# A small local attention with 64 patch units per core, rewritten inside a four-layer kernel

## What is computed

```python
q = Wq @ qp + bq;  k = Wk @ qp + bk;  val = Wv @ vp + bv          # 64 x 128 a patch
scores = einsum('bhdi,bhdj->bhij', qh, kh) / sqrt(8)
scores = where(mask > 0, scores, -1e9);  attn = softmax(scores)
o = gelu(einsum('bhij,bhdj->bhdi', attn, vh))                     # exact gelu
out = (Wo @ o + bo) * masks
```

## Time and profile before

| | us |
|---|---|
| median of 3 runs | 3458.11 (3456.35 to 3464.62) |
| profiled execution, its own time | 3458.61 |
| its span | 3456.7 |
| PE busy | 3137.7 (91%) |
| DVE busy | 1975.3 (57%) |
| POOL busy | 1141.7 (33%) |
| ACT busy | 943.9 (27%) |

### The profile page before, as it was taken

The page is one execution under the profiler, slowest core; times in us unless marked ns, Lnnn a source line. Parts: engine busy times, 40 slices in busy tenths (PEclk is TensorE's granted clock), DMA queues, the critical chain, the costliest instruction groups (busy, mean ns, idle before and its releaser), DMA issues.

```text
span 3456.7 us, 47231 instructions
## 1 busy us (share of the span) xinstructions
PE 3137.7 (91%) x15840; PEld 2524.9 (73%) x15840; DVE 1975.3 (57%) x3823; ACT 943.9 (27%) x3176; POOL 1141.7 (33%) x935
## 2 busy tenths in 40 slices
PE   5999999999989889989989888888878999999899
PEld 4778888888768644457767677777766888888687
DVE  7555555555543454477766666666666444445643
ACT  2222222222210033310033333333322333333211
POOL 4333333433255222136621221222113322232264
PEclk9999999999999965579999999999989999999999
DMA  2111111111111000021110110110002111111011
GB/s 97 40 40 42 36 39 45 45 42 36 44 43 39 18 20 13 7 60 31 41 34 19 28 30 18 30 30 24 9 22 58 29 35 30 30 38 29 26 51 46
DMA packets 68604, 120.64 MB, mean 35 GB/s; under 512 B 7840, under 2 KB 13216, under 8 KB 68112
## 3 DMA queue, kind: packets, MB, share of 16 engines
q1 hardware_dynamic: 68496, 119.23, 11.6%
HBM read 117.11 MB, written 2.10 MB: 34 GB/s over the span
## 4 chain that ended last, share of the span: by engine, by line
PE 71%; DVE 17%; issue 6%; ACT 3%; POOL 2%; DVEq 0%; DMA 0%; POOLq 0%; ACTq 0%; SPq 0%
PE proj L341 31%; PE outp L341 18%; PE heado L823 5%; PE score L803 4%; PE score L1593 3%; PE turn L816 2%; DVE nw_t L370 2%; PE score L341 2%; DVE nw_t L368 1%; DVE tbuf L988 1%; PE turn L742 1%; ACT sq L897 1%; DVE x L1038 1%; DVE rowmax L993 1%; DVE stats L390 1%
## 5 line engine op out<-in xcount | busy, mean ns | idle before, releaser
L341 PE MATMUL outp<-w_out,acts 128*128 128x512 f32 x3288 | 867.8, 408 | 38.0 <-DVE x L1038 20.0
L341 PE MATMUL proj<-xnT,w_in 128*128 128x512 f32 x3288 | 783.5, 393 | 9.5 <-DVE big L864 3.0
L341 PEld LDWEIGHTS outp<-w_out,acts 128*128 128x128 f32 x3288 | 607.8, 193 | 176.3 <-DVE x L1038 29.4
L341 PEld LDWEIGHTS proj<-xnT,w_in 128*128 128x128 f32 x3288 | 613.8, 189 | 141.7 <-issue 6.3
L341 PE MATMUL proj<-ctxT,w_kv 128*128 128x512 f32 x2304 | 563.4, 404 | 52.9 <-DVE big L864 43.7
L341 PEld LDWEIGHTS proj<-ctxT,w_kv 128*128 128x128 f32 x2304 | 443.0, 194 | 153.6 <-DVE big L864 46.6
L602 POOL TENSOR_TENSOR w_out<-ring,consts 128x512 fp32r<-128x512 f32 x96 | 104.0, 1083 | 1039.8 <-PE outp L341 1039.8
L1038 DVE TENSOR_TENSOR x<-x,outp 128x512 f32<-128x512 f32 x384 | 261.4, 686 | 255.6 <-PE outp L341 254.1
L913 ACT ACTIVATE pbuf<-tbuf,negmax 128x128 f32<-128x128 f32 x512 | 199.2, 390 | 396.9 <-DVE negmax L995 393.9
L602 POOL TENSOR_TENSOR w_kv<-ring,consts 128x512 fp32r<-128x512 f32 x96 | 105.8, 1102 | 465.0 <-DMA ring<-in_L_wk 465.0
L864 DVE COPY big<-proj 128x512 f32<-128x512 f32 x136 | 94.0, 691 | 255.7 <-PE proj L341 255.3
(11 more groups left out here) (239 smaller groups left out, 4032.7 us busy)
## 6 DMA issues: line engine op xcount, KB each, us to landing
ring<-in_L_wq SPq DMA_DIRECT2D x96, 256.0 KB, 2.7
ring<-in_L_wo SPq DMA_DIRECT2D x96, 256.0 KB, 2.6
ring<-in_F_in SPq DMA_DIRECT2D x52, 256.0 KB, 2.6
ring<-in_L_wk SPq DMA_DIRECT2D x48, 256.0 KB, 2.7
ring<-in_L_wv SPq DMA_DIRECT2D x48, 256.0 KB, 2.8
ring<-in_F_out SPq DMA_DIRECT2D x41, 256.0 KB, 2.6
ring<-in_mask SPq DMA_DIRECT2D x16, 256.0 KB, 3.2
x<-in_x SPq DMA_DIRECT2D x2, 1024.0 KB, 7.4
```

What stands on the lines that cost most here:

```text
L341: mm = pe.matmul(bank_ap, w_ap(a, c), rhs(b, c), start=first and c == 0 and n == 0, stop=last and c == chunks - 1 and n == len(PASSES) - 1)
```

## The change

- **Scores.** q and k are projected three times over into stacks of 96 rows for each s (`wq3`, `wk3`: 4 projections a batch instead of 2). The stack holds high, high, low of q against high, low, high of k, so that one fp32r pass over 98 rows gives the score. Two rows hold the mask.
- **Softmax.** DVE takes the negated maximum, and ACT takes four exps a unit, straight from PSUM with the maximum as bias. The subtraction goes.
- **Values.** The stationary operand is a 128x128 block: 8 value rows per head on a diagonal, and 8 columns of ones. All 8 heads accumulate into one PSUM column block per patch. The result is channels by positions already, with 64 rows of values and 64 rows of sums. Turning back, copying out and per-patch scaling go; DVE takes one reciprocal of 64x512 a batch and one product of 64x512. The copies out of `turn` are shared: ACT for even units, DVE for odd.
- **Key tiles.** POOL writes 98x512 tiles for each unit into 8 buffers. It also clears the padded value blocks ahead of the stage.
- **End.** Gelu, mask (POOL) and `Wo` with its bias as row 65 go batch by batch. Nothing is turned. DVE adds once.
- **F1's start.** SP loads F1's first weights once the last batch's keys are masked. POOL splits them (`ffn_pool_first`) before its tail work. `c2` of F1 has a place of its own.
- The loops over batches are written out instead of running on a register.

The core of the diff (added lines; what is removed is in the listing above; `...` marks left-out lines; in `kraw1`, `kstk`, `qstk`, `kbd`, `v1`, `sum1` the first index after the rows is the buffer):

```diff
+        wait(pool, m["blocked"], UNITS * b)
+        for s in range(2):
+            pool.wait_ge(m["k_high"], 2 * b + s + 1)
+            pool.tensor_tensor(kstk[32:64, b % 2, s, :], kraw1[32:64, s, :], kstk[32:64, b % 2, s, :].bitcast(F32),
+                               ALU.subtract).then_inc(m["k_low"], 1)
+        pool.wait_ge(m["mask_made"], 2 * b + 2)
+        pool.wait_ge(m["k_low"], 2 * b + 2)
+        for u in range(UNITS):
+            n, s = divmod(u, 2)
+            wait(pool, m["sfull"], UNITS * (b - 1) + u + 1)
+            pool.tensor_tensor(kbd[0:ROWS, u, :].rearrange("p (h j) -> p h j", h=4),
+                               kstk[0:ROWS, b % 2, s, n * P:(n + 1) * P].bitcast(F32).unsqueeze(1)
+                               .broadcast_to([ROWS, 4, P]), heads, ALU.mult).then_inc(m["blocked"], 1)
...
+    def project_k(b, s):
         pe.wait_ge(m["normed"], b + 1)
...
+        if s == 0:
+            wait(pe, m["v_made"], b)
+        else:
+            wait(pe, m["q_low"], 2 * b)
+        pe.matmul(proj[s][0:STACK, :], wk3[:, s * STACK:(s + 1) * STACK], xn1[b % 2], start=True, stop=True)\
+          .then_inc(m["k_full"], 1)
...
+    def project_q(b, s):
+        pe.wait_ge(m["k_masked"], 2 * b + s + 1)
+        pe.matmul(proj[s][0:STACK, :], wq3[:, s * STACK:(s + 1) * STACK], xn1[b % 2], start=True, stop=True)\
+          .then_inc(m["q_full"], 1)
...
...
+    def scores(u):
+        b, n, s = u // UNITS, u % UNITS // 2, u % 2
+        pe.wait_ge(m["blocked"], u + 1)
+        pe.wait_ge(m["q_low"], 2 * b + s + 1)
+        wait(pe, m["exps"], u - 1)
+        pe.matmul(score[s][:, :], qstk[0:ROWS, b % 2, s, n * P:(n + 1) * P], kbd[0:ROWS, u % UNITS, :],
+                  start=True, stop=True).then_inc(m["sfull"], 1)
...
+    def turn_probabilities(u):
+        s = u % 2
+        pe.wait_ge(m["exps"], u + 1)
+        wait(pe, m["tfree", s], u // 2)
+        for h in range(4):
+            mm = pe.transpose(turn1[s][:, h * P:(h + 1) * P], pbuf[:, s, h * P:(h + 1) * P], ident)
+        mm.then_inc(m["tfull"], 1)
...
+    def values(u):
+        b, n, s = u // UNITS, u % UNITS // 2, u % 2
+        if u % UNITS == 0:
+            pe.wait_ge(m["v_made"], b + 1)
+            wait(pe, m["onorm"], b - 1)
+        pe.wait_ge(m["tfree", s], u // 2 + 1)
+        for h in range(4):
+            e = (4 * s + h) * P
+            mm = pe.matmul(sum1[b % 2][:, n * P:(n + 1) * P], v1[:, b % 2, n, e:e + P],
+                           ptbuf[:, s, h * P:(h + 1) * P], start=s == 0 and h == 0, stop=s == 1 and h == 3)
+        mm.then_inc(m["av"], 1)
...
+    def extras(b, i):
+        if b + 1 >= B:
+            return
+        if i < 2:
+            project_k(b + 1, i)
+        elif i < 4:
+            project_q(b + 1, i - 2)
+        elif i == 5:
+            project_v(b + 1)
...
+    for s in range(2):
+        project_k(0, s)
+    for s in range(2):
...
     def out_product(b):
...
+        if b == 1:
+            pe.wait_ge(m["onorm"], B)
+        pe.wait_ge(m["weighed"], b + 1)
+        wait(pe, m["added"], b - 1)
...
+    def high_of_keys(b, s):
+        act.wait_ge(m["k_masked"], 2 * b + s + 1)
+        wait(act, m["blocked"], UNITS * (b - 1))
+        act.activation(kstk[0:STACK, b % 2, s, :], kraw1[0:STACK, s, :], ACT.Copy).then_inc(m["k_high"], 1)
...
+    def high_of_queries(b, s):
+        act.wait_ge(m["q_full"], 2 * b + s + 1)
+        wait(act, m["sfull"], UNITS * (b - 1))
+        act.activation(qstk[0:STACK, b % 2, s, :], proj[s][0:STACK, :], ACT.Identity, bias=bq3[0:STACK, s:s + 1])\
+           .then_inc(m["q_high"], 1)
...
+    def exps(u):
+        s = u % 2
+        act.wait_ge(m["rowmax"], u + 1)
+        wait(act, m["tfull"], u - 1)
+        for h in range(4):
+            a = act.activation(pbuf[:, s, h * P:(h + 1) * P], score[s][:, h * P:(h + 1) * P], ACT.Exp,
+                               bias=negmax[:, s, h:h + 1])
+        a.then_inc(m["exps"], 1)
...
+    def take_turned(u):
         act.wait_ge(m["tfull"], u + 1)
         wait(act, m["av"], u - 1)
...
...
+    def extras(b, i):
+        if b + 1 >= B:
+            return
+        if i in (1, 2):
+            high_of_keys(b + 1, i - 1)
+        elif i in (3, 4):
+            high_of_queries(b + 1, i - 3)
...
+    F0.events.wait(act, "outfull", B * ((F0.chunks + 1) // 2))
...
+    def norm(b):
+        wait(dve, m["q_full"], 2 * b - 2)
+        dve.tensor_scalar(xn1[b % 2], x[:, b, :], moments[:, b, 0:1], rstd[:, b:b + 1], ALU.subtract, ALU.mult)\
+           .then_inc(m["normed"], 1)
...
+    def mask_keys(b):
+        dve.wait_ge(m["mask_landed", b % 2], 16 * (b // 2 + 1))
+        dve.wait_ge(m["w_made"], 3)
+        wait(dve, m["k_masked"], 2 * b)
+        row = ring[:, 2 + b % 2, :]
+        dve.tensor_scalar(live1, row[0:STACK, :], 0.0, None, ALU.is_gt).then_inc(m["mask_made"], 1)
+        wait(dve, m["blocked"], UNITS * (b - 1))
+        dve.tensor_scalar(kstk[STACK:ROWS, b % 2, :, :], row[STACK:ROWS, :].unsqueeze(1).broadcast_to([2, 2, D]), 0.0,
+                          consts[STACK:ROWS, C_HEADS + 4:C_HEADS + 5], ALU.is_le, ALU.mult).then_inc(m["mask_made"], 1)
...
+    def take_keys(b, s):
+        dve.wait_ge(m["k_full"], 2 * b + s + 1)
+        dve.wait_ge(m["mask_made"], 2 * b + 1)
+        wait(dve, m["k_low"], 2 * (b - 1) + s + 1)
+        dve.scalar_tensor_tensor(kraw1[0:STACK, s, :], proj[s][0:STACK, :], bk3[0:STACK, s:s + 1], live1, ALU.add,
+                                 ALU.mult).then_inc(m["k_masked"], 1)
...
+    def low_of_queries(b, s):
+        dve.wait_ge(m["q_high"], 2 * b + s + 1)
+        dve.scalar_tensor_tensor(qstk[64:STACK, b % 2, s, :], proj[s][64:STACK, :], bq3[64:STACK, s:s + 1],
+                                 qstk[64:STACK, b % 2, s, :].bitcast(F32), ALU.add, ALU.subtract).then_inc(m["q_low"], 1)
...
+    def take_values(b):
+        dve.wait_ge(m["v_full"], b + 1)
+        dve.wait_ge(m["padded"], 2 * min(b + 1, 2))
+        wait(dve, m["av"], UNITS * (b - 1))
+        made = proj[0][:, 0:PATCH * E1].rearrange("p (n h d) -> p n h d", n=PATCH, h=H1)
+        for h, block in enumerate(diagonal_blocks(b % 2, 0)):
+            one = dve.tensor_copy(block, made[:, :, h, :])
+        one.then_inc(m["v_made"], 1)
...
+    def maxima(u):
+        s = u % 2
         dve.wait_ge(m["sfull"], u + 1)
...
         wait(dve, m["exps"], u - 1)
...
...
+    def take_turned(u):
+        dve.wait_ge(m["tfull"], u + 1)
+        wait(dve, m["av"], u - 1)
+        dve.tensor_copy(ptbuf[:, 1, :], turn1[1][:, :]).then_inc(m["tfree", 1], 1)
...
+    def normalise(b):
+        dve.wait_ge(m["av"], UNITS * (b + 1))
+        wait(dve, m["onorm"], b)
+        dve.reciprocal(inv1, sum1[b % 2][E1:2 * E1, :]).then_inc(m["inverted"], 1)
+        dve.wait_ge(m["inverted"], b + 1)
+        dve.tensor_tensor(o1[b], sum1[b % 2][0:E1, :], inv1, ALU.mult).then_inc(m["onorm"], 1)
...
+    def extras(b, i):
+        if i == 3 and b:
+            normalise(b - 1)
+        if b + 1 < B:
+            if i < 2:
+                take_keys(b + 1, i)
+            elif i in (4, 5):
+                low_of_queries(b + 1, i - 4)
+            elif i == 6:
+                take_values(b + 1)
+        if b + 2 < B:
+            if i == 6:
+                norm(b + 2)
+            elif i == 7:
+                mask_keys(b + 2)
...
+    norm(0)
```

More of the change, by code:

```diff
@@ L1139, in ffn_sp, with ffn_pool_tiles @@
             ffn_run(sp, A, chunks)
-        def ffn_pool(pool, A):
+        def ffn_pool_tiles(pool, A, g, j):
             m = A.events
[L1145 to L1189, removed]
@@ L1526, in l1_pool @@
-            in_pairs(pool, batch)
+            F0.events.wait(pool, "sfull", 2 * F0.chunks)
+            for k in range(2):
+                pool.memset(v1[:, k, :, :], 0.0).then_inc(m["padded"], 1)
+                pool.wait_ge(m["padded"], 2 * k + 1)
+                for block in diagonal_blocks(k, E1):
+                    one = pool.memset(block, 1.0)
+                one.then_inc(m["padded"], 1)
+            F0.events.wait(pool, "outfull", B * ((F0.chunks + 1) // 2))
+            pool.wait_ge(m["padded"], 4)
@@ new lines, in l1_pe @@
+            for u in range(UNITS * B):
+                scores(u)
+                extras(u // UNITS, u % UNITS)
+                if u >= 2:
+                    turn_probabilities(u - 2)
+                if u >= 3:
+                    values(u - 3)
+            u = UNITS * B
+            turn_probabilities(u - 2)
+            values(u - 3)
+            turn_probabilities(u - 1)
+            values(u - 2)
+            values(u - 1)
+            def out_product(b):
+                if b == 1:
+                    pe.wait_ge(m["onorm"], B)
+                pe.wait_ge(m["weighed"], b + 1)
+                wait(pe, m["added"], b - 1)
+                pe.matmul(outp[b % 2][:, :], wo1, flat[0:E1 + 1, b * D:(b + 1) * D], start=True, stop=True)\
+                  .then_inc(m["out_full"], 1)
@@ L1677, in l1_act @@
```

(30 more changed lines are left out.)

404 lines of the change are left out of this document (152 added, 252 removed).

## The result

The changed kernel takes 3366.86 us (median of 4 runs, 3363.91 to 3370.65), the kernel before 3457.75 in runs on the same chip. The ratio is 0.9734, 95% interval 0.9717 to 0.9751: **91 us faster**, where 41 was forecast. The time lies inside the range.

The account below looks back on a forecast made before the run. It took TensorE at half clock to bound the small attention. Middle -22 and end -14 summed to -36, up to -46; it took -41 from 3458.1, so 3417 us, range 3355 to 3452.

Parts of the forecast that it names:

- What bounds the kernel: Small attention: TensorE at half clock, 93% busy, with a 3.2 us idle stretch in each 34.3 us batch.
- TensorE's work: Small attention, per batch: 18.3 us at the higher clock, 33.8 at the lower; old batch without its gap 31.
- The reciprocal: DVE's new 64x512 reciprocal in `normalise`: taken as 4.4 us, between bounds of 0.69 and 4.36.
- rival A: Small attention: reciprocal streams in about 0.7 us or the gap leaves the clock up; 3360 us, chance 0.22.
- The gap: TensorE idles 4.6 us ahead of the value projection, waiting for DVE behind `normalise`; the clock then falls.
- The step that failed: Middle batches: clock stays low after the gap until the next batch's projections; 30 us a batch, 180 for batches 1 to 6.
- if the clock rises at once: Upper end of the summed gain: up to -46 us instead of -36.
- First and last batch: Batch 0, without `normalise`, 22 to 26 us; batch 7, without projections to raise the clock, 31 us.
- The start and the end: First maximum at about 1211, 3 us either way; F1's first product about 14 us earlier from the last value product.
- The end's terms, -10 and -5: Stage end: output batches at 1.75 us instead of 3.0, -10; Newton steps and low-rank product freed of POOL, -5.
- the term for clearing the padded blocks: Clearing the padded value blocks: no row of its kind, counted as nothing.
- Rival B: Small attention: the clock never comes back, all at 1.2 GHz; 3469 us, slower, chance 0.09.

Follow-up runs that it names:

- experiment 1: Kernel before, with the masking of the next batch's keys moved behind the maxima of unit 3 instead of unit 2: 3358.36 us against 3454.54.
- experiment 2: Changed kernel with the 64x512 reciprocal of a batch made a plain copy of the same shape: 3334.40 us, ratio 0.9649.
- experiment 11: Changed kernel with value products side by side (sums left out) and plain float32 scores over 65 rows: ratio 0.9871.
- experiment 12: Changed kernel with F1's weights fetched and split only once the first output product is done: ratio 0.9756.
- experiments 9 and 10: 9: changed kernel, side-by-side value products (sums left out), float32 scores over 98 rows, 0.9752. 10: changed kernel, nine-column value products, float32 scores over 65 rows, 0.9857.
- experiment 4: Changed kernel with the score product in plain float32 over the same 98 rows: ratio 0.9796.
- experiment 3: Changed kernel with the 64x512 reciprocal cut into four 64x128 pieces behind the maxima of four units: 3338.68 us, ratio 0.9664.

## Why the prediction was right in kind and half in size

- **What bounds the kernel**: right, and shown by experiment 1. The gap that the earlier trace rows show, and the clock behind it, cost 95 us.
- **TensorE's work**: 18.3 us a batch at the high clock; experiment 2, with a gap of 1.0 us and no low clock, takes 19.5. A score's row is 0.53 us in the mean and not 0.21 or 0.41 (from its start to the next product's 0.31 us at the high clock and 0.57 at the low one; the 0.41 came from a group of the earlier trace rows over which the clock was 0.60 in the mean, and not 0.50). A plain unit is 1.57 us instead of 1.7, one with a projection 2.43 instead of 2.65.
- **The reciprocal**: 3.36 us for a forecast of 4.36. The slope of the earlier trace rows was too steep: pieces of 128 elements take 0.96, so an element costs (3.36 - 0.96) / 384 = 6.25 ns and not 8.25. The Trainium skill's "VectorE: DVE Perf Modes", "First, the fixed hardware budget", has the divide iterate; a copy of this shape runs in 0.70 (experiment 2), so the rule agrees with the row in kind, and rival A is out.
- **The gap**: 3.67 for 4.6 us, in the place foretold, once in each batch. The 1.0 us is the reciprocal's.
- **The step that failed**: "Then at the lower clock: values 1.8, rest of unit 5 2.7, units 6 and 7 3.1 each ... Unit 0 of the next batch brings values, score and projection in a row". I took from the old trace that plain units never raise the clock, and only projections do. That was true of the old products and not of the new: the clock came back in unit 6, 6 us after the gap instead of 11 to 14. Six batches took 142.4 us instead of 180. Experiment 11 puts the old products back and gets 30.8 us a batch. The terms added up to -36; the forecast of -41 stood midway to the -46 "if the clock rises at once", so an early return was priced at 10 us in all, where these six batches alone came out 38 us shorter. The argument used the new products' durations with the old products' effect on the clock.
- **First and last batch**: 18.5 us for 24 and 23.2 for 31. The first has neither `normalise` nor its gap and stands close to TensorE's 18.3 us; the prediction gives no working for its 24. The last batch has no projections, and the clock came back there too: the same error. With the six batches in between, these make the 51 us by which the middle part was off.
- **The start and the end**: 3.6 us earlier for 3 either way, and 14.5 for 14. The end's terms, -10 and -5, add up to 15 where the prediction counted 14. Of the 5 us put to POOL and the Newton steps, experiment 12 shows 3.3. No row of the kernel before shows the term for clearing the padded blocks, which the prediction put at nothing. That came out right: POOL cleared them in two instructions of 3.5 us from 1167 to 1175 us, ahead of the stage.
- **Rival A** priced a clock that stays up at 3360. Its time was near, for another reason: there was a gap, and the clock did fall. **Rival B** had the clock never come back. The Trainium skill's "TensorE: Matmul & The Clock Gate", "Part 4: PE-mode transpose", has the full clock not engage for transposes, which do not count as busy in the same way. Here the clock came back in units in which they take 0.44 of 1.57 us (at the higher clock), so that rule doesn't decide this stage.

## What to carry to other kernels

Before a stage is rebuilt, look for the one wait that precedes each fall of TensorE's clock, and try moving it: here one line of the old kernel was worth the whole rebuild, and in the rebuilt kernel four pieces for one long instruction gave another 24 us. When a change alters the products, what the trace shows of the clock's return under the old ones doesn't carry over; give both cases a chance and a time.

## What the runs showed of the hardware that I had not expected

- Four value products of 8 or 9 columns take 0.41 us to four groups of partitions and 1.04 to 1.09 us to the same ones; 9, 64 or 128 columns make little difference (1.04, 1.09 and 1.06).
- A float32 score took 0.96 us to the next product's start at the high clock when the value product ahead of it had 8 or 9 stationary columns (experiments 9 and 10), and 0.86 behind one with 128 (experiment 4).
- The same idle stretch of 1.5 us was followed by a fall of the clock in some batches and not in others of one execution (experiment 3).
- With a plain float32 score over 98 rows the clock was up for longer, 0.97 against 0.88 over the middle part (experiment 4). TensorE had more to do and idled less, 2.4 us instead of 3.7; which of the two did it was not separated.
- Side by side, float32 scores over 65 and over 98 rows took the same 1.12 us at the high clock, and the low stretch of a repeated batch was 17 to 20.5 us with the one and 3.5 with the other (experiments 11 and 9).
